# A decoder layer on one core: feed-forward transposes and all behind them four steps later, a third buffer for their input, softmax sums copied one unit earlier

## What is computed

```python
x = x + self_attention(layernorm(x))             # windowed, 16 heads, grouped output projection
x = x + cross_attention(layernorm(x), ctx)       # 16 heads over 1024 keys, ALiBi slopes, mask
h = layernorm(x)                                 # the feed-forward part, 2048 rows
gate = act_quant(h) @ weight_quant(w_gate).T     # 512 -> 2048, activations to 8 bits per row
up   = act_quant(h) @ weight_quant(w_up).T
f    = silu(gate) * up
x    = x + act_quant(fwht(f)) @ weight_quant(w_down).T   # Walsh-Hadamard transform over 2048
```

## Time and profile before

| | us |
|---|---|
| median of 3 runs | 1639.65 (1635.01 to 1639.69) |
| the profiled execution, own time | 1639.33 |
| its span in the profile | 1637.5 |
| self-attention and the start of cross-attention | 0 to about 640 |
| cross-attention | to 1322.7 |
| feed-forward | 1322.7 to 1637.5 |

### The profile page before, as it was taken

How to read it: one execution, slowest core, us unless ns; L and a number is a source line. 1 busy time by engine, 2 the same in 40 slices (tenths; PEclk the granted TensorE clock), 3 DMA queues, 4 the chain that set the end, 5 groups by cost and what they waited for, 6 DMA issues and landing times. The chain is left out here.

```text
span 1637.5 us, 23915 instructions
## 1 busy us (share of the span) xinstructions
PE 1555.2 (95%) x7487; PEld 1070.2 (65%) x7520; DVE 1224.0 (75%) x2240; ACT 1185.7 (72%) x1962; POOL 1271.3 (78%) x1142
## 2 busy tenths in 40 slices
PE   8899999999999988999999999999999969999996
PEld 3478777877787755666566666666656526666664
DVE  2489989878877756787877788778888556767765
ACT  2355556777755435999999889989998837878875
POOL 0387787787777714899989999999999938888880
PEclk9999999999999998999999999999999999999999
DMA  7224241433330105211312032102202130100100
GB/s 247 105 65 101 70 92 56 109 123 115 117 114 15 33 22 153 58 45 26 107 39 63 20 106 61 33 20 48 69 13 87 75 115 1 40 27 26 33 14 26
DMA packets 57190, 110.24 MB, mean 67 GB/s; under 512 B 9244, under 2 KB 13596, under 8 KB 56682
## 3 DMA queue, kind: packets, MB, share of 16 engines
q1 hardware_dynamic: 55488, 107.64, 22.2%
q10 hardware_dynamic: 1578, 1.07, 0.2%
HBM read 71.26 MB, written 18.88 MB: 55 GB/s over the span
## 5 line engine op out<-in xcount | busy, mean ns | idle before, releaser
L1421 POOL TENSOR_TENSOR x_p_lo<-x_p,x_p_hi 128x1024 fp32r<-128x1024 f32 x256 | 606.3, 2396 | 62.5 <-ACT x_p_hi L1201 39.4
L1334 DVE TENSOR_REDUCE x_maxes<-x_ps_a 128x1 f32<-128x1024 f32 x252 | 306.6, 1217 | 121.2 <-PE x_ps_a L1521 117.0
L1164 ACT ACTIVATE x_p<-x_ps_b,x_any_valid 128x1024 f32<-128x1024 f32 x256 | 285.0, 1113 | 58.5 <-PE x_ps_b L1501 53.8
L1201 ACT ACTIVATE x_p_hi<-x_p 128x1024 fp32r<-128x1024 f32 x256 | 271.2, 1059 | 6.3
L1501 PE MATMUL x_ps_b<-x_Q,x_K 103*128 103x512 f32 x512 | 218.9, 509 | 7.2 <-ACT x_p L1164 5.6
L1555 PE MATMUL x_ps_o<-x_p_hi,x_V 128*96 128x512 f32 x512 | 208.9, 408 | 2.5 <-POOL x_p_lo L1421 2.5
L1556 PE MATMUL x_ps_o<-x_p_lo,x_V 128*96 128x512 f32 x512 | 201.6, 394 | 0.0
L1521 PE MATMUL x_ps_a<-x_K,x_Q 99*128 99x512 f32 x504 | 166.8, 412 | 11.4 <-DVE x_maxes L1334 8.4
L443 ACT ACTIVATE a_aT_hi<-a_ps_a 128x512 fp32r<-128x512 f32 x64 | 38.3, 598 | 175.1 <-PE a_ps_a L726 142.0
L1501 PEld LDWEIGHTS x_ps_b<-x_Q,x_K 103*128 103x128 f32 x512 | 88.2, 191 | 98.1 <-issue 56.0
L1521 PEld LDWEIGHTS x_ps_a<-x_K,x_Q 99*128 99x128 f32 x504 | 88.5, 190 | 54.5 <-DVE x_maxes L1334 32.1
(11 more groups left out here) (286 smaller groups left out, 4000.9 us busy)
## 6 DMA issues: line engine op xcount, KB each, us to landing
shared<-in_L_ffn_w_gate SPq DMA_DIRECT2D x16, 512.0 KB, 4.2
shared<-in_L_ffn_w_up SPq DMA_DIRECT2D x16, 512.0 KB, 4.1
shared<-in_L_ffn_w_down SPq DMA_DIRECT2D x16, 512.0 KB, 4.4
shared<-in_ctx SPq DMA_DIRECT2D x8, 1024.0 KB, 7.6
x_scratch<-rows SPq DMA_DIRECT2D x31, 256.0 KB, 2.0
x_Q<-x_q_hi SPq DMA_DIRECT2D x112, 64.0 KB, 2.0
shared<-in_L_attn_out_w SPq DMA_DIRECT2D x6, 1024.0 KB, 8.4
ffn_quant<-shared SPq DMA_DIRECT2D x24, 256.0 KB, 4.4
```

Source lines behind the costliest of these rows:

```text
L1164: act.activation(p[:, v % 3, :, :], ps_b[:, :, :], ACT.Exp, scale=any_valid[:, b % 2:b % 2 + 1]).then_inc(exp_ready, 1)
L1201: act.activation(p_hi[:, r], p[:, v % 3], ACT.Copy).then_inc(hi_ready, 1)
L1334: dve.tensor_reduce(out=maxes[:, c % 2, 3 + r:4 + r], in_=scores_bank(n)[:, :, :], axis=mybir.AxisListType.XY, op=ALU.max).then_inc(max_re ...
L1421: pool.tensor_tensor(out=p_lo[:, v % 3], in0=p[:, v % 3], in1=p_hi[:, r].bitcast(F32), op=ALU.subtract).then_inc(lo_ready, 1)
```

## The change

- In the feed-forward the transposes of `fB` and everything behind them (`fT_hi`, `fT_lo`, `ps_z`, `zr`, `quantise`, `zq` transposes, down, output) move four steps later: the lags 6, 7, 8, 9, 11 to 14 and 17 become 10, 11, 12, 13, 15 to 18 and 21. The loop gets four more steps. Since four steps are one tile, every operation keeps its place within a step.
- `fB` gets three buffers, the row tiles `xt` eight.
- The Hadamard conversion on ACT moves from step 1 to step 5.
- SP loads the row tiles ahead of `wd`, and waits for the last stored rows only before it loads these.
- In cross-attention the copy of the sums (`sums`) moves from r = 1 to r = 0 of the same head; the addition stays.
- The last four matmuls of `last_out` move from the units (HEADS, 0) and (HEADS, 1) to (HEADS, 2), behind the last product with V.
- The preparation of the first feed-forward row tile moves: statistics from (62, 3) to (60, 3), deviation from (63, 0) to (61, 1), bias from (63, 1) to (62, 0), normalisation on ACT from (63, 2) to (62, 3), its maximum from (63, 3) to (63, 2).

```diff
@@ -921,7 +921,7 @@
-                    (HEADS, 0): ((2, 0), (2, 1)), (HEADS, 1): ((2, 2), (2, 3))}
+                    (HEADS, 2): ((2, 0), (2, 1), (2, 2), (2, 3))}
@@ -1182,7 +1182,7 @@
-                if (c, r) == (HEADS - 1, 2):
+                if (c, r) == (HEADS - 2, 3):
@@ -1269,12 +1269,15 @@
-            def numerator(k):
+            def sums(k):
...
+            def numerator(k):
+                j, G = k % HPG, k // HPG
@@ -1338,6 +1341,8 @@
+                if r == 0 and c >= 2:
+                    sums(c - 2)
@@ -1352,17 +1357,17 @@
-                if (c, r) == (HEADS - 2, 3):
+                if (c, r) == (HEADS - 4, 3):
...
-                if (c, r) == (HEADS - 1, 1):
+                if (c, r) == (HEADS - 2, 0):
...
-                if (c, r) == (HEADS - 1, 3):
+                if (c, r) == (HEADS - 1, 2):
@@ -1378,6 +1383,7 @@
+            sums(HEADS - 1)
@@ -1423,7 +1429,7 @@
-                if (c, r) == (HEADS - 1, 0):
+                if (c, r) == (HEADS - 3, 1):
@@ -1596,7 +1602,7 @@
-XR = 7
+XR = 8
@@ -1645,7 +1651,7 @@
-        fB = sb("fB", [P, 2, F])
+        fB = sb("fB", [P, 3, F])
@@ -1681,7 +1687,7 @@
-        steps = range(-1, NQ + 18)
+        steps = range(-1, NQ + 22)
@@ -1709,9 +1715,9 @@
-            if n >= 2:
-                eng.wait_ge(fT_made, 4 * (n - 1))
-            eng.tensor_tensor(out=fB[:, n % 2, half * 1024:(half + 1) * 1024], in0=fA[:, 0:1024], in1=fA[:, 1024:],
+            if n >= 3:
+                eng.wait_ge(fT_made, 4 * (n - 2))
+            eng.tensor_tensor(out=fB[:, n % 3, half * 1024:(half + 1) * 1024], in0=fA[:, 0:1024], in1=fA[:, 1024:],
@@ -1719,15 +1725,16 @@
-            sp.dma_start(wd[:, :, :], ffn_quant[2].rearrange("p (c n) -> p c n", c=FC)).then_inc(ffn_in[2], 16)
-            for j in range(3):
-                sp.wait_ge(x2_stored[j], 16 * 5)
...
+            sp.dma_start(wd[:, :, :], ffn_quant[2].rearrange("p (c n) -> p c n", c=FC)).then_inc(ffn_in[2], 16)
...
+                    if n + XR > TPB * (B - 1):
+                        sp.wait_ge(x2_stored[(n + XR) % 3], 16 * 5)
@@ -1750,17 +1757,17 @@
-                if c == 1:
+                if c == 5:
...
-                if quarter(c, 6):
-                    act.wait_ge(fT_made, c - 5)
-                    if quarter(c, 8):
-                        act.wait_ge(z_made, c - 7)
+                if quarter(c, 10):
+                    act.wait_ge(fT_made, c - 9)
+                    if quarter(c, 12):
+                        act.wait_ge(z_made, c - 11)
...
-                if i == 1 and quarter(c, 13):
-                    m = (c - 13) // 4
+                if i == 1 and quarter(c, 17):
+                    m = (c - 17) // 4
@@ -1788,16 +1795,16 @@
-                if i == 0 and quarter(c, 12):
-                    quantise((c - 12) // 4, 1)
-                if quarter(c, 7):
-                    m, j = quarter(c, 7)
-                    act.wait_ge(z_made, c - 6)
+                if i == 0 and quarter(c, 16):
+                    quantise((c - 16) // 4, 1)
+                if quarter(c, 11):
+                    m, j = quarter(c, 11)
+                    act.wait_ge(z_made, c - 10)
...
-                if i == 3 and quarter(c, 11):
-                    m = (c - 11) // 4
+                if i == 3 and quarter(c, 15):
+                    m = (c - 15) // 4
@@ -1809,8 +1816,8 @@
-                if i == 1 and quarter(c, 17):
-                    m = (c - 17) // 4
+                if i == 1 and quarter(c, 21):
+                    m = (c - 21) // 4
@@ -1827,8 +1834,8 @@
-                if i == 1 and quarter(c, 9) or i == 3 and quarter(c, 11):
-                    m, half = (c - 9) // 4, i // 2
+                if i == 1 and quarter(c, 13) or i == 3 and quarter(c, 15):
+                    m, half = (c - 13) // 4, i // 2
@@ -1851,16 +1858,16 @@
-                if i == 2 and quarter(c, 14):
-                    m = (c - 14) // 4
+                if i == 2 and quarter(c, 18):
+                    m = (c - 18) // 4
...
-                if quarter(c, 6):
-                    dve.wait_ge(fT_hi_ready, c - 5)
-                    if quarter(c, 8):
-                        dve.wait_ge(z_made, c - 7)
+                if quarter(c, 10):
+                    dve.wait_ge(fT_hi_ready, c - 9)
+                    if quarter(c, 12):
+                        dve.wait_ge(z_made, c - 11)
@@ -1922,21 +1929,21 @@
-                if quarter(c, 6):
-                    m, j = quarter(c, 6)
+                if quarter(c, 10):
+                    m, j = quarter(c, 10)
...
-                    if quarter(c, 8):
-                        pe.wait_ge(fT_lo_ready, c - 7)
+                    if quarter(c, 12):
+                        pe.wait_ge(fT_lo_ready, c - 11)
...
-                        last = pe.transpose(ps_t[c % 2][:, a * P:(a + 1) * P], fB[:, m % 2, (4 * j + a) * P:(4 * j + a + 1) * P],
+                        last = pe.transpose(ps_t[c % 2][:, a * P:(a + 1) * P], fB[:, m % 3, (4 * j + a) * P:(4 * j + a + 1) * P],
...
-                    if m >= 4:
-                        pe.wait_ge(zqT_ready, 2 * (m - 3))
+                    if m >= 5:
+                        pe.wait_ge(zqT_ready, 2 * (m - 4))
@@ -1953,8 +1960,8 @@
-                if quarter(c, 7):
-                    k = c - 7
+                if quarter(c, 11):
+                    k = c - 11
@@ -1966,8 +1973,8 @@
-                if i == 0 and quarter(c, 12) or i == 1 and quarter(c, 13):
-                    m = n - 3
+                if i == 0 and quarter(c, 16) or i == 1 and quarter(c, 17):
+                    m = n - 4
@@ -1976,8 +1983,8 @@
-                if quarter(c, 13):
-                    m, j = quarter(c, 13)
+                if quarter(c, 17):
+                    m, j = quarter(c, 17)
```

## The result

Before: 1639.67 us, median of 4 runs (1635.01 to 1640.22). After: 1629.61 us, median of 4 (1628.75 to 1629.78). The ratio is 0.9942, 95% interval [0.9926, 0.9958]: faster by 9.5 us (6.9 to 12.1). The forecast was 1632.4 in a range of 1628 to 1638.5: right in sign and inside the range, 2.8 us too slow. The profiled executions are 1639.33 and 1629.57, which makes 9.76 us to place.

The account below looks back on a forecast made before the run. PE was taken to bound the feed-forward to within 0.6 us a tile. Terms -5.0 + 0.2 - 1.95 - 1.0 = -7.75, plus 0.8 for the clock, took 1639.33 to 1632.4 us; range 1628 to 1638.5.

Parts of the forecast that it names:

- Hadamard conversion, -5.0: Feed-forward start: with the conversion in step 5, ACT's silu of step 1 no longer waits for `had_raw`; 5.0 us gained.
- SP's loads, 0: Feed-forward start: row tiles loaded ahead of `wd` bring `had_raw` no earlier and change nothing; 0 us.
- The lag, +0.2: Feed-forward pipeline: extra steps at start and drain cost 6.1 us, 5.9 come back; +0.2 us net.
- 22.11 to the end stay: Feed-forward drain: the stretch from the last transposes to the end keeps its 22.11 us.
- Cross-attention's end, -1.95: Last projections behind the last product with V: the clock is kept and residual additions run without waits; 1.95 us gained.
- The sums, -1.0: Cross-attention: copying the sums at r = 0 shortens PE's waits for DVE's row maxima; 1.0 us gained, bounds +1 and -4.
- rival (B): Cross-attention: splitting the sums frees the ring and gives all of 4 us, not 1; 1629.4 us, chance 0.10.
- The first row tile, 0: Cross-attention's last heads: preparing the first feed-forward row tile two heads earlier is the same operations; 0 us, bounds 0 and +2.
- (A): PE's clock falls in light steps and at cross-attention's end and nothing hides it; 1635.6 us, chance 0.20.
- The 0.8 that I added: Feed-forward start: 0.8 us added, as the clock can fall in the four additional light steps.
- (C): Feed-forward start and drain: each of eight light steps costs a steady step's 4.4 us or more; 1646 us, chance 0.08.
- (D): Feed-forward: the changed waits were hidden anyway, and the 5.0 us come back in a later wait; 1637.4 us, chance 0.10.

## Why the prediction was right, step by step

**Hadamard conversion, -5.0.** The size is right: step 3's gate is 8.64 behind the phase's start, 13.81 before, so 5.17. The stretch of low clock in step 7 is another matter: it is in the profile before and not in those of the sums and the last projections alone, with the same feed-forward, so it was a feature of one execution. I had priced it at 1.6 and counted it among the lag's gains. The load was covered, as forecast: the conversion in step 5 waits for nothing.

**SP's loads, 0.** Right as a term beside the other, wrong as a reading. I wrote that the order would bring `had_raw` no earlier. It brings it in 3.6 and 4.2 us in place of 8.49 and 8.7, and by itself gives 6.9 us in the median and 5.7 to the last transposes. The sum came out right because the moved conversion had already taken the same wait. The Trainium skill (Trainium Kernel Development and Optimization, Key Constraints) says that DMAs issued by SP and by ACT interleave on the same 16 engines. The trace bears out that they share something, since one queue's load is delayed by the other's; the step from there to "no earlier" was mine, and the runs contradict it.

**The lag, +0.2.** Most pieces hold. (The bounds are mis-added: with the steady gain of 2.0 kept and every other piece at its own bound they are -5.9 and +11.4, not -5 and +13.) To step 7: 1.1 less than with `had` moved alone (20.99 against 22.07), forecast 1.1. Steps 7 to 11: 10.42, forecast 10.7. Steps 11 to 15: 13.86, forecast 13.9; but of the gain of 2.9, 1.4 comes without the lag too (15.33 to 15.35 in the five profiles of kernels without it whose clock stays up there), and 1.5 is the lag's, most of it the wait for `fB`. A steady tile: 17.40, forecast 17.42. Steps 68 to 72: 12.82, forecast 13.0. Beside `had` moved alone the lag makes -1.1 + 10.4 - 1.5 - 2.1 - 17.6 + 12.8 = +0.9; measured to the last transposes +1.1 (287.09 to 286.01) and +0.9 (286.90), and +2.3 (288.34) where the clock fell in the light steps. The ends of the pipeline cost 23.2, and a tile's worth of steady work and three small gains pay back 22.3. Beyond that lies the clock at the end, a term whose "22.11 to the end stay" was off by 2.2 in the profiled execution and right in the repeated one. In the five profiles of kernels with the lag and without extra matmuls that stretch is 22.0 twice, and 23.4, 24.1 and 24.3. The medians put the lag at 2.7 us over the same kernel without it.

**Cross-attention's end, -1.95.** Measured -2.04, in company with the other two edits. Alone it shows -0.44 in its stretch, the forecast's value for a low clock, and nothing in the median. The agreement is in part luck: 0.4 is the order of the matmuls, and the other 1.6 is a stretch of low clock that was in the profile before and is missing in one of four profiles of the same code.

**The sums, -1.0: the step that was mis-sized.** In the whole change the stretches in which they act give 3.59 from 735 to 1199 and 0.73 more to the last `p_lo`: 4.3, a little over my bound of 4. Alone they give 4.0 there. I priced them at a small part of PE's waits for the row maxima and argued that POOL is the slower. The waits of the kernel after, from 800 to 1200 us, read

```profile
PE x_ps_a L1527 <- DVE x_maxes L1337: 1.1, 2, 0.7
```

in place of 4.6 in twelve waits. That is 3.5 less in a stretch in which the whole kernel gained 3.1 (3.59 x 400 / 463), so close to all of what PE no longer waits reaches POOL and the end. POOL's groups on the page say the same: its idle time ahead of `p_lo` fell from 62.5 to 58.8. The row before is

```profile
L1421 POOL TENSOR_TENSOR x_p_lo<-x_p,x_p_hi 128x1024 fp32r<-128x1024 f32 x256 | 606.3, 2396 | 62.5 <-ACT x_p_hi L1201 39.4
```

and the one after

```profile
L1427 POOL TENSOR_TENSOR x_p_lo<-x_p,x_p_hi 128x1024 fp32r<-128x1024 f32 x256 | 606.1, 2395 | 58.8 <-ACT x_p_hi L1201 32.8
```

POOL's own 606 us are the same to 0.2. So POOL, though the slowest on average here, still had idle time, and nearly all of the stall upstream of it came through. This was rival (B), with 0.10 and 1629.4; its mechanism is the one that came true. That its total fits to 0.2 us as well owes something to luck, since other terms were off and cancelled.

**The first row tile, 0.** Right. The cover ahead of DVE was 1.2 by my working. In order of time, and by DMA issue:

```profile
1257.54 1.13 SPq L1067 DMA_DIRECT2D shared<-x_scratch  x2
...
1271.98 0.64 DVE L1364 BATCH_NORM_STATS2 x_stats<-shared 128x6 f32<-128x512 f32 x1
```

```profile
shared<-x_scratch SPq DMA_DIRECT2D x2, 256.0 KB, 13.6
```

The load lands at 1271.1 (1257.54 + 13.6), some 0.8 ahead of `bn_stats`, which has no wait in brackets. That is thin cover, but cover.

**The other rivals.** (A) was half right: the clock did fall and nothing hid it, in the first profile behind PE's wait of 3.57 in the drain. In the light steps at the start it stayed up there and in the repeated run, but fell in the runs with two buffers and with extra matmuls, at 1.2 us each. The 0.8 that I added for this is thus near the 0.6 that two executions in four at 1.2 come to. (C) is refuted: four light steps take 10.42 at the start and 12.82 in the drain, 2.6 and 3.2 each where it needed 4.5. (D) is refuted: the 5.0 are still there at the end.

**What the sum comes to.** The sums gave 3.3 more than forecast and the cross-attention's end 0.1 more; the feed-forward gave 3.3 where -5.0 + 0.2 + 0.8 = -4.0 was forecast; 0.1 came from the stretches before. 1632.4 - 3.3 - 0.1 + 0.7 - 0.1 = 1629.6. That the feed-forward comes within 0.7 is luck in part: the kernel after loses 2.2 to the clock in its drain, the kernel before 1.4 in step 7, and a second execution of the kernel after does without the 2.2.

**Open.** Why the granted clock falls in one execution and not in the next of the same code, behind the same wait; and whether the moved projections keep it up or only came with it.

## What to carry to other kernels

When a change has several parts, time it both ways, each part added alone and each taken out of the whole: here two edits removed the same wait, and one (the longer lag) hid a loss of 2.7 us by the medians behind the others' gain, so that the change without it, 1626.96 us, beats both kernels. A longer lag in a software pipeline is paid at both ends: price its fill and its drain (23.2 us here) against the steady gain times the number of tiles (2.1) and the tile that drops out, before building it. Before a stretch is credited to an edit, look for it in other profiles of the same code: here two stretches of low clock, 1.4 and 1.6 us, came and went without any edit. And don't discount a wait because another engine is slower on average; look whether that engine has idle time ended by the chain that waits.

## What the runs showed of the hardware

The duration of a small load depends on what another queue has just issued: 256 KB on ACT's queue took 8.5 to 8.8 us where SP's queue had a load of 2 MB first (six profiles), and 3.6 to 4.4 where it had loads of 256 KB first (eight).

TensorE's granted clock fell to its lower level (1.2 GHz) behind waits of some 3.1 to 3.6 us and in light steps, but not each time. Behind the same wait of 3.57 us it was low from 1615.65 to 1622.5 in one execution of the kernel after and nowhere in the feed-forward in the other; with the same wait of 3.10 at the end of cross-attention it was low in three profiles of the same code and stayed up in a fourth. The cost depended on how long it lasted and on what came next: 2.2 us where 6.8 us of low clock met the last 16 matmuls, and nothing in the kernel without the lag, where a stretch of 3.4 us began 11.4 us ahead of the end and the last transposes were still 22.0 from it.

The stretch to the multiplication at 735 took from 731.86 to 736.06 us in six profiles of the same code, while the 463 us of cross-attention behind it repeated to within 0.15. The largest part of the spread between these profiles, 4.2 us, thus arises before 735; the stretch of the feed-forward to the last transposes has 2.0.
